# Last part of a graph block: two finishing steps of a group on GpSimd and two on VectorE, none on ScalarE

## The reference

```
x = layernorm(x + attention(x, adj, adj))     # 16 heads, Wq Wk Wv Wo, bias adj+adj, softmax
x = layernorm(x + experts(x, adj))            # router picks one of 4 experts for a graph
                                              # adj @ (x @ W), batch norm over all graphs of
                                              # the expert, gamma, beta, relu
layernorm(x) = (x - mean) / sqrt(var + 1e-5)  # over the 512 features
```

## Time and profile before

| | |
|---|---|
| median of 3 runs | 2743.18 us (2741.02 to 2743.3) |
| profiled execution, its own time | 2744.08 us |
| its span in the trace | 2742.3 us |
| last part, from the first load of its constants at 2476.77 us | 265.5 us |
| busy in the whole span: TensorE / VectorE / ScalarE / GpSimd | 94% / 77% / 65% / 32% |

### The profile page before, as it was taken

One profiled execution on the slowest core, in us unless ns is written; L12 is line 12 of the kernel. 1 busy time (PEld: TensorE's weight loads), 2 busy tenths in 40 slices (PEclk: granted clock), 3 DMA queues, 4 the chain that ended last, 5 costly groups with the idle time before them and its releaser, 6 DMA issues. The chain is left out here.

```text
span 2742.3 us, 61258 instructions
## 1 busy us (share of the span) xinstructions
PE 2581.8 (94%) x20290; PEld 2156.2 (79%) x20290; DVE 2103.7 (77%) x4095; ACT 1782.1 (65%) x6184; POOL 889.1 (32%) x491
## 2 busy tenths in 40 slices
PE   7899999999999999999999999999999999867755
PEld 6788888888888888888888888888888888756644
DVE  5977877877877877877877877877877877844977
ACT  4666666666666666666666666666666666635986
POOL 1132332322322332332322322332332321123776
PEclk9999999999999999999999999999999999987887
DMA  5544544544544544544544544544544544458997
GB/s 214 188 162 180 193 162 171 192 164 170 192 163 178 193 164 177 193 164 170 192 164 170 192 166 176 191 166 176 192 166 169 191 164 165 174 203 327 426 417 307
DMA packets 155053, 540.32 MB, mean 197 GB/s; under 512 B 17586, under 2 KB 50354, under 8 KB 107698
## 3 DMA queue, kind: packets, MB, share of 16 engines
q1 hardware_dynamic: 154802, 536.96, 52.8%
HBM read 427.84 MB, written 109.05 MB: 196 GB/s over the span
## 5 line engine op out<-in xcount | busy, mean ns | idle before, releaser
L604 ACT ACTIVATE prob<-prob,neg_max 128x128 f32<-128x128 f32 x2048 | 792.4, 394 | 5.8 <-DVE abs_max L733 5.8
L370 POOL TENSOR_TENSOR norm<-norm,constants 128x1 f32<-128x1 f32 x128 | 70.5, 551 | 1430.8 <-DVE norm L779 1430.8
L604 ACT ACTIVATION_READ_ACCUMULATOR prob<-prob,neg_max 128x1 f32 x2048 | 396.0, 193 | 0.0
L360 POOL TENSOR_TENSOR moments<-moments,conv 128x1024 f32 x128 | 308.9, 2413 | 267.5 <-ACT conv L655 230.4
L590 ACT ACTIVATE qk<-bank 128x512 f32<-128x512 f32 x256 | 152.8, 598 | 319.2 <-PE bank L379 319.2
L705 DVE SCALAR_TENSOR_TENSOR prob<-bank,adj_in 128x512 f32<-128x512 f32 x512 | 316.9, 681 | 11.2 <-PE bank L379 11.2
L722 DVE TENSOR_TENSOR prob<-prob,inv_sum 128x2048 f32<-128x2048 f32 x128 | 295.7, 2310 | 4.4
L728 DVE TENSOR_REDUCE neg_max<-prob 128x16 f32<-128x2048 f32 x128 | 291.8, 2280 | 0.0
L733 DVE TENSOR_REDUCE abs_max<-prob 128x16 f32<-128x2048 f32 x128 | 291.6, 2278 | 0.0
L597 ACT ACTIVATE probT<-bank 128x512 f32<-128x512 f32 x512 | 265.2, 609 | 26.6 <-PE bank L430 26.6
L346 POOL TENSOR_TENSOR xT_lo<-xT_in,xT_hi 128x1024 fp32r<-128x1024 f32 x62 | 274.9, 4433 | 5.0
(11 more groups left out here) (135 smaller groups left out, 5891.3 us busy)
## 6 DMA issues: line engine op xcount, KB each, us to landing
expert_hi<-expert_hi_scratch SPq DMA_DIRECT2D x125, 1024.0 KB, 4.8
expert_lo<-expert_lo_scratch SPq DMA_DIRECT2D x125, 1024.0 KB, 6.9
x_in<-x SPq DMA_DIRECT2D x128, 256.0 KB, 2.6
x_scratch<-x SPq DMA_DIRECT2D x128, 256.0 KB, 2.4
conv_scratch<-conv SPq DMA_DIRECT2D x128, 256.0 KB, 3.0
conv_in<-conv_scratch SPq DMA_DIRECT2D x32, 1024.0 KB, 9.6
x_in<-x_scratch SPq DMA_DIRECT2D x32, 1024.0 KB, 12.3
out<-x_in SPq DMA_DIRECT2D x32, 1024.0 KB, 13.2
```

The lines of the kernel that those rows point to most:

```text
L360: pool.tensor_tensor(acc, acc, conv[:, :, :].rearrange("p k d -> p (k d)"), ALU.add).then_inc(moments_added, 1)
L604: last = act.activation(prob[:, par2, h, :], prob[:, par2, h, :], ACT.Exp, bias=neg_max2[:, par2, h:h + 1], scale=2.0, accum_out=row_sum[: ...
```

## The change

ScalarE no longer takes a turn; its function for a group only scales, and its loop no longer runs two groups longer. VectorE's `finish` does turns 2 and 3 with the same instruction, waits for nothing of ScalarE and forms no shift. SP's store waits for GpSimd's two and VectorE's two steps. GpSimd's wait before it overwrites rstd (two buffers) is on VectorE's steps instead of ScalarE's.

```diff
--- before.py
+++ after.py
@@ -823,7 +823,7 @@
     NG = B // G
     RING = 8 if NG % 8 == 0 and NG > 8 else 4
     REFILL_LAG = 1
-    POOL_TURNS, ACT_TURN, DVE_TURN = 2, 2, 3
+    POOL_TURNS = 2
     assert NG % RING == 0 and NG > RING and G == 4 and C == 4 and G * ROWS == P
 
     def sb(name, shape, dt=F32):
@@ -852,7 +852,6 @@
     mean_var = sb("mean_var2", [P, 2, G, 2])
     var_eps = sb("var_eps2", [P, 2, G])
     rstd = sb("rstd2", [P, 2, G])
-    shift = sb("shift2", [P, 2, G])
     ps_turned, ps_back = bank[4:8], bank[0:4]
 
     ld_bn = sem("ld_bn")
@@ -874,9 +873,7 @@
     var_ready = sem("var_ready2")
     rstd_made = sem("rstd_made2")
     rstd_seen = sem("rstd_seen")
-    shift_made = sem("shift_made2")
     pool_finished = sem("pool_finished")
-    act_finished = sem("act_finished")
     dve_finished = sem("dve_finished")
 
     def run_groups(eng, group, lag):
@@ -918,8 +915,7 @@
             g = k * RING + r
             if live(g):
                 sp.wait_ge(pool_finished, (g + 1) * POOL_TURNS)
-                sp.wait_ge(dve_finished, g + 1)
-                sp.wait_ge(act_finished, g + 1)
+                sp.wait_ge(dve_finished, (g + 1) * (G - POOL_TURNS))
                 sp.dma_start(by_token(out, g * G, G), flat(x1_in, r)).then_inc(st_g[r], 16)
             h, r1 = g - REFILL_LAG, (r - REFILL_LAG) % RING
             if live(h) and live(h + RING):
@@ -986,7 +982,7 @@
             g = k * RING + r
             pool.wait_ge(var_ready, g + 1)
             if live(g - 2):
-                pool.wait_ge(act_finished, g - 1)
+                pool.wait_ge(dve_finished, (g - 1) * (G - POOL_TURNS))
             pool.tensor_tensor(rstd[:, r % 2, :], var_eps[:, r % 2, :], minus_half[:, :].to_broadcast([P, G]),
                                ALU.pow).then_inc(rstd_made, 1)
             pool.wait_ge(rstd_made, g + 1)
@@ -1021,14 +1017,8 @@
                     last.then_inc(scaled, 1)
                     if r < RING - 1:
                         ahead.append(expert(g + 1, c))
-            h, r2 = g - 2, (r - 2) % RING
-            if live(h):
-                act.wait_ge(shift_made, h + 1)
-                act.activation(x1_in[:, r2, ACT_TURN, :], x1_in[:, r2, ACT_TURN, :], ACT.Identity,
-                               bias=shift[:, r2 % 2, ACT_TURN:ACT_TURN + 1],
-                               scale=rstd[:, r2 % 2, ACT_TURN:ACT_TURN + 1]).then_inc(act_finished, 1)
-
-        run_groups(act, group, 2)
+
+        run_groups(act, group, 0)
 
     @block.vector
     def _(dve):
@@ -1074,13 +1064,9 @@
         def finish(g, r, live):
 
             dve.wait_ge(rstd_made, g + 1)
-            if live(g - 2):
-                dve.wait_ge(act_finished, g - 1)
-            dve.scalar_tensor_tensor(out=shift[:, r % 2, :], in0=mean_var[:, r % 2, :, 0], scalar=-1.0,
-                                     in1=rstd[:, r % 2, :], op0=ALU.mult, op1=ALU.mult).then_inc(shift_made, 1)
-            dve.tensor_scalar(x1_in[:, r, DVE_TURN, :], x1_in[:, r, DVE_TURN, :], mean_var[:, r % 2, DVE_TURN, 0:1],
-                              rstd[:, r % 2, DVE_TURN:DVE_TURN + 1], ALU.subtract,
-                              ALU.mult).then_inc(dve_finished, 1)
+            for j in range(POOL_TURNS, G):
+                dve.tensor_scalar(x1_in[:, r, j, :], x1_in[:, r, j, :], mean_var[:, r % 2, j, 0:1],
+                                  rstd[:, r % 2, j:j + 1], ALU.subtract, ALU.mult).then_inc(dve_finished, 1)
 
         def take_stats(h, r, j):
             dve.wait_ge(joined, h * G + j + 1)
```

## The result

The changed kernel takes 2745.54 us in the median of 17 runs, the kernel before 2741.48 us in 17 runs on the same chips. The ratio is 1.0015, with a 95% interval from 1.0009 to 1.0022: 4.1 us slower, 2.5 to 6.0. Two of the 17 executions of the changed kernel, 3156 and 4286 us at granted clocks of 0.785 and 0.562, were slow ones, and the ratio leaves them out (the median of the other 15 is 2745.37 us). The move is inside the 0.2% band that the prediction called no change (5.5 us; the interval reaches just beyond it), and the time is inside its range. The point was 2745.0 us, but against a median of 2743.18 us, so it meant +1.8 us; the measured move is +4.1.

What follows compares the result with a forecast made beforehand. The prediction took DMA, at 7.37 us a group, to bound the last part. First refill 0.7 plus tail 1.1 gave +1.8 us on a median of 2743.18, hence 2745.0 us; range 2739.5 to 2750.

Steps and rivals of the forecast that it cites:

- VectorE's two steps: VectorE loses the shift and gains a second step: +0.39 to +0.58 us a group, 6.78 us a group in bursts.
- DMA sets the pace: In the last part DMA needs 7.37 us a group, more than the compute engines, so ScalarE's dropped steps gain nothing.
- The tail: After the last load nothing hides VectorE's longer steps and GpSimd's slower last pair: +1.1 us, bounds 0.8 and 1.5.
- VectorE then does groups 30 and 31 without a rest: After the last load lands, VectorE works through the final two groups, whose longer steps add 0.95 us.
- The first refill: At the loop's entry the first refill follows a later store of group 1: +0.7 us, bounds 0.3 and 1.6.
- The sum: First refill 0.7 plus tail 1.1 gives +1.8 us for the whole kernel.
- The loop's boundary: Between loop iterations ScalarE's lead nearly covers its 8.20 us stand; an iteration takes 55 to 58 us, costing 0.
- rival A: Loop boundary not covered, an iteration 62.4 us against DMA's 59.0: slower, put at 2750 us; chance 0.20.
- ScalarE's waits: The DMA queue's 70.3 us of waiting for ScalarE's step looks like the prize but is not.
- rival B: Store waits on ScalarE's step are real: faster, 2739.4 us, or 2736 with half the slow spells gone; chance 0.12.
- The shared port: VectorE and GpSimd share a port, where a later operation would block; the prediction held that its trace rows disagree.
- rival C: VectorE's second step waits 2.15 us for a GpSimd step, 8.3 us a group: 2778 us; chance 0.02.

Runs made afterwards that it cites:

- The shortened GpSimd: The changed kernel with GpSimd's two finishing steps doing 4 of 512 columns: 2736.33 us, ratio 0.9980 to the kernel before.
- the wait without the work: Changed kernel with VectorE doing turn 2 only and stores also waiting for ScalarE's scaling of group g+2: 2739.86 us, ratio 0.9995 to the kernel before.
- steps early: The changed kernel with VectorE's two finishing steps moved behind the statistics of turn 0: 2742.37 us, ratio 0.9999 to the kernel before.
- steps late: The changed kernel with VectorE's two finishing steps moved behind the statistics of turn 3: 2740.69 us, ratio 0.9998 to the kernel before.

## Why the prediction was right in its range and wrong in its main term

The time fell in the range and the class was right (no change by 0.2%). The way there was partly another. That the point, 2745.0 us, lies 0.5 us from the measured median is luck: the median of 3 runs that it stood on was 1.7 us above that of 17, and the move was +4.1 us, not +1.8.

- **VectorE's two steps**: the term that was mis-sized. The prediction took 0.64 us for the second step as for the first and put the upper bound of the addition at +0.58 us a group. Measured are 7.20-6.20 = 1.00 us. The row it rested on the earlier trace rows it read as a step in the middle of GpSimd's. GpSimd's steps there start at 2513.67 and 2515.74 us, so that step began 1.64 us into the first and ended 0.29 us into the second: it too lay at the passage, only later than the new first step. The new second step has another place, 0.22 us into GpSimd's second, for which the prediction had no row. The shortened GpSimd brings the pair to 0.90 us, other places to 1.09 and 1.20.
- **"DMA sets the pace"**: true of the kernel before, no longer of the changed one. 7.20 us are still under DMA's 7.37, and the refills come no faster than that (7.6 us apart in the mean). But VectorE's first join comes 28.9 us after the first load in either kernel, and from there to its group 31 the changed kernel takes 2724.54-2504.24 = 220.3 us (in both profiles), with no idle moment over 0.4 us; the kernel before takes 219.5 and 217.4 us, with waits in them. By an estimate from these rows, 31 groups at the forecast 6.78 us come to 210 us, which leaves a reserve; at 7.20 us it is used up, and VectorE is the bound. With the last load landing 12 us sooner nothing moved.
- **The tail**: forecast +1.1 us (bounds 0.8 and 1.5). Measured from TensorE's start on the last load: 31.5 and, in the second profile, 29.8 us, against 27.1 and 2740.5-2713.67 = 26.8. That is +2.7 to +4.7. The step that failed is "VectorE then does groups 30 and 31 without a rest": it is still behind when the last load comes, and starts group 31 13.8 us (2724.54-2710.72) and 12.2 us later, against 10.9 and 10.6. From there to the end it is 17.7 us against 16.3, +1.4, where the terms of group 31 and of GpSimd's last pair came to +0.7.
- **The first refill**: forecast +0.7 us. From the first load's issue the first refill went out at 2523.18-2475.31 = 47.9 us, against 2524.60-2477.64 = 47.0: +0.9, as described. But it did not reach the end: the last load came no later, 235.4 and 237.0 us against 235.8 and 237.5.
- **The sum**: by the means of two profiles of each kernel, -0.4 for the last load and +3.7 behind it are +3.3 us; the medians have +4.1 (2.5 to 6.0).
- **The loop's boundary** (rival A): ScalarE still stands there, 5.04 us as the profile counts it, and VectorE is idle 0.37 us. Its lead covers the stand, as forecast, and the iterations take 57.8 and 57.2 us, inside the forecast 55 to 58. VectorE's own boundary, for which up to 3 us were allowed, is in these 0.37 (0.34 at group 24).
- **ScalarE's waits** (rival B): the wait without the work costs nothing, so the step of the prediction holds that calls the 70.3 us of the earlier trace rows no prize. The prediction's sign for this rival, a last load more than 2 us earlier, did show in the first profiles (235.4 against 237.5); the second ones (237.0 and 235.8) take it back. The slow spells of DMA are still there in every profile (366 to 379 GB/s from 2664 to 2696 us in the changed kernel); their cause stays open.
- **The shared port** (rival C): its chance was 0.02 and its price far off, 2.15 us a step, but the kind of mechanism is the one that made the difference. The Trainium skill (SBUF — State Buffer, Who interferes with whom) says that the later of the two engines blocks until the other's instruction has ended. The runs bear out the waiting, in both directions, but not that VectorE waits for the whole instruction: a VectorE step that starts 1.24 us into GpSimd's takes 0.53 us, the time it takes alone, and no delay of one was above 0.45 us. The prediction saw +0.16 us in its rows and dismissed the rule. By the whole rule the step of the earlier trace rows would have waited 2515.74-2515.31 = 0.43 us, so that row lay near the end of GpSimd's step and could say little of other places.

## What to carry to other kernels

A duration taken beside another engine's work holds for the phase in which it was taken: before a second such instruction is priced like the first, look where the other engine's single instructions begin and end at its new place; a row that draws two as one hides it. Where an engine at 6.2 us a group stands beside a bound of 7.4, count what it has left after the last load too, since a backlog there is paid in full. The long wait of the DMA queue was no prize here, with the DMA engines full and the issue in time. And a bracket that names who ended a wait is to be held against the count that the wait asks for.

## What the runs showed of the hardware

A finishing step of 128x512 float32 on VectorE takes 0.54 us, and 0.45 us from start to start, with GpSimd quiet. GpSimd's step of the same form takes 2.08 us alone. Beside each other both can get longer, and by how much depends on where one starts in the other. Some steps one by one (timelines of a single engine in narrow windows), first steps early:

```profile
2591.90 2.08 POOL L991 TENSOR_SCALAR x_in<-x_in,mean_var,rstd 128x512 f32<-128x512 f32 x1 [0.21 <-POOL rstd L986]
2592.23 0.71 DVE L1068 TENSOR_SCALAR x_in<-x_in,mean_var,rstd 128x512 f32<-128x512 f32 x1
2592.86 0.53 DVE L1068 TENSOR_SCALAR x_in<-x_in,mean_var,rstd 128x512 f32<-128x512 f32 x1
```

Then steps late, and the last group of the changed kernel, where VectorE's first step (2733.04 us) is there before GpSimd's:

```profile
2591.88 2.24 POOL L991 TENSOR_SCALAR x_in<-x_in,mean_var,rstd 128x512 f32<-128x512 f32 x1
2593.12 0.53 DVE L1068 TENSOR_SCALAR x_in<-x_in,mean_var,rstd 128x512 f32<-128x512 f32 x1
2593.57 0.82 DVE L1068 TENSOR_SCALAR x_in<-x_in,mean_var,rstd 128x512 f32<-128x512 f32 x1
...
2733.21 2.61 POOL L991 TENSOR_SCALAR x_in<-x_in,mean_var,rstd 128x512 f32<-128x512 f32 x1 [0.21 <-POOL rstd L986]
2733.50 0.54 DVE L1068 TENSOR_SCALAR x_in<-x_in,mean_var,rstd 128x512 f32<-128x512 f32 x1
```

VectorE's delayed steps end at one of two moments only. In all the profiles with whole GpSimd steps, each VectorE step of over 0.6 us beside GpSimd (344 of them) ends either 1.04 us before the end of a GpSimd step or 0.28 us after it, wherever it started. So a step that starts 0.33 us into GpSimd's ends 1.04 us into it (0.71 us long), and one that starts 1.52 or 1.64 us into it ends 2.36 us from its start (0.84 or 0.72 us long). Steps that start about 0.5 to 1.3 us into it are not delayed.

In the other direction GpSimd's step grows when VectorE is the one that came first. A VectorE step that runs until 1.49 us into GpSimd's costs it nothing; one that runs until 1.77 us lengthens it from 2.08 to 2.24 us (steps late), until 1.82 us to 2.29. One that still runs at its start and ends 0.3 us into it makes it 2.23 us, as in the changed kernel, and two VectorE steps across its start make it 2.61 us, without being delayed themselves.

This looks as if the two took turns at something that VectorE's step holds for its whole length and GpSimd's only for some tenths of a us behind its start and again before its end. That reading fits the rows shown; what is held was not tested.
